# Last block of a graph network: softmax denominators inverted with nodes on partitions, self products moved into the edge loop's drain, batch statistics by rounds

## The reference, cut to what matters

```python
h = jnp.maximum(_layernorm(x, axis=-1), 0.0)
...
ex = jnp.exp(attn - amax[edge_src])
denom = jax.ops.segment_sum(ex, edge_src, num_segments=n)
alpha = ex / (denom[edge_src] + 1e-16)
upd = jax.ops.segment_sum(v * alpha[..., None], edge_src, num_segments=n)
upd = upd.reshape(n, OV) @ W_out
out = tfn_features @ W_self + upd
mu = out.mean(axis=0)
var = out.var(axis=0)
return (out - mu) * jax.lax.rsqrt(var + EPS_BN) * gamma + beta
```

## Time and profile before

| what | us |
|---|---|
| median of 3 timed runs (lowest, highest) | 3129.48 (3127.07, 3130.35) |
| span of the profiled execution, first to last instruction | 3126.1 |
| time of the profiled execution outside the span | not listed |
| busy: PE, DVE, POOL, ACT | 2476.7, 2209.2, 2032.3, 864.2 |
| from the last accumulation into acc to the end of the span | 64.3 |

### The profile page before, as it was taken

How to read it: one execution, slowest core, us unless ns; L and a number is a source line. 1 busy time by engine, 2 the same in 40 slices (tenths; PEclk the granted TensorE clock), 3 DMA queues, 4 the chain that set the end, 5 groups by cost and what they waited for, 6 DMA issues and landing times. The chain is left out here.

```text
span 3126.1 us, 51454 instructions
## 1 busy us (share of the span) xinstructions
PE 2476.7 (79%) x14006; PEld 2130.6 (68%) x14006; DVE 2209.2 (71%) x5060; ACT 864.2 (28%) x2414; POOL 2032.3 (65%) x2119
## 2 busy tenths in 40 slices
PE   5778787525667667477777767999999999999986
PEld 4777787424666666355555556888888888888862
DVE  4555555526888887555555563888888888888875
ACT  1111111136666663111111110222232222323231
POOL 4777777457777771277777736777776677677710
PEclk9776667657888888599999978999999999999985
DMA  3443333133333330155555557889888898888820
GB/s 84 94 89 86 86 87 86 30 68 64 61 60 60 60 52 4 46 155 160 152 160 152 160 147 179 214 206 214 212 206 205 203 216 206 207 204 205 213 68 11
DMA packets 333760, 404.38 MB, mean 129 GB/s; under 512 B 171136, under 2 KB 203006, under 8 KB 333570
## 3 DMA queue, kind: packets, MB, share of 16 engines
q1 hardware_dynamic: 252034, 251.20, 34.4%
q0 software_dynamic: 66560, 96.41, 14.5%
q10 hardware_dynamic: 14976, 54.53, 5.1%
HBM read 339.81 MB, written 62.07 MB: 129 GB/s over the span
## 5 line engine op out<-in xcount | busy, mean ns | idle before, releaser
L1934 PE MATMUL psum<-ckv,z 128*128 128x256 f32 x4160 | 967.8, 383 | 0.0
L1934 PEld LDWEIGHTS psum<-ckv,z 128*128 128x128 f32 x4160 | 766.7, 191 | 97.9
L1768 POOL DMA_INDIRECT acc<-QW,dst_i x416 | 399.5, 960 | 184.6 <-issue 111.2
L234 POOL DMA_INDIRECT ga<-TA,src_i x416 | 412.4, 991 | 161.6 <-issue 126.5
L1789 POOL DMA_INDIRECT ga<-XX,src_i x416 | 399.5, 960 | 162.8 <-issue 122.5
L1027 POOL DMA_INDIRECT ga<-T,src_i x416 | 401.9, 966 | 151.5 <-issue 125.9
L234 POOL DMA_INDIRECT ga<-T,src_i x416 | 396.6, 953 | 149.3 <-issue 124.7
L2048 DVE TENSOR_TENSOR z<-psum,shb 128x2560 f32<-128x2560 f32 x104 | 293.2, 2820 | 66.7 <-PE psum L1925 66.5
L1121 PE MATMUL psum<-HT,wy 128*128 128x128 f32 x1664 | 264.7, 324 | 70.0 <-DVE wy L1394 69.2
L445 PE MATMUL psum<-wre,re 128*128 128x68 f32 x832 | 215.2, 351 | 119.4 <-DVE oneT L290 67.7
L1121 PEld LDWEIGHTS psum<-HT,wy 128*128 128x128 f32 x1664 | 242.8, 232 | 87.8 <-DVE wy L1394 81.5
(11 more groups left out here) (362 smaller groups left out, 4142.9 us busy)
## 6 DMA issues: line engine op xcount, KB each, us to landing
shb<-in_ea SPq DMA_DIRECT2D x104, 640.0 KB, 6.2
WKV<-wkvo ACTq DMA_DIRECT2D x104, 512.0 KB
shb<-in_ea SPq DMA_DIRECT2D x104, 512.0 KB, 8.5
wkv<-WKV SPq DMA_DIRECT2D x104, 512.0 KB
dl<-DL SPq DMA_DIRECT2D x208, 128.0 KB
win<-TB SPq DMA_DIRECT2D x416, 32.0 KB
ga<-T,src_i POOLq DMA_INDIRECT x832
ef<-in_ea SPq DMA_DIRECT2D x104, 128.0 KB
```

The lines of the kernel that those rows point to most:

```text
L234: pool.indirect_dma_start(o, None, table, bass.IndirectOffsetOnAxis(ap=src_i[:, g * GT + t:g * GT + t + 1], axis=0)).then_inc(s_g[k], 16)
L1768: pool.indirect_dma_start(qg[:, (g % QR) * GT + t, :], None, QW, bass.IndirectOffsetOnAxis(ap=dst_i[:, g * GT + t:g * GT + t + 1], axis=0) ...
L1934: last = pe.matmul(kv_of(k)[:, t, :], z[:, k % 2, j, t * 128:(t + 1) * 128], ckv[:, j, :], start=(j == 0), stop=(j == NZ - 1))
```

## The change: what it does

The end of the fourth block is rewritten, and two things move into the edge loop's drain.

- The denominators are transposed: PE turns each of the 25 blocks of 24x125 into 125x24, with nodes on partitions (banks 1 and 7). DVE adds the three parts with one reduction per bank, adds 1e-16 and takes the reciprocal of 125x200 elements in two pieces (8 and 17 blocks). ACT writes each value 16 times in a row, round by round (`widened`), and PE transposes these blocks of 125x128 back into PSUM (banks 6 and 7), where DVE multiplies acc by them (`scaled`). sel_b, its building on POOL and its copies are gone.
- The w_self products get a bank each and are issued ahead (`own_product`): numbers 0 to 4 in the drain, at the end of PE's steps k = 1 to 5, number 5 after the reductions, number 6 in the last round. They leave the accumulation open for w_out.
- In the drain, steps without softmax work do `values` between the two halves of `add_sums`.
- DVE takes batch statistics of each round as its OT copy is done (`bn_stats`) and combines them (`bn_aggr`). A shift is worked out too, so that ACT scales and shifts OT by rounds into Y, from which PE transposes, into seven banks, without waiting for DVE's additions to X.
- ACT takes a square and a square root at the start of the end.

```diff
@@ edge loop, PE: body, and own_product ahead of it
+                def own_product(n):
+                    a, w = CH[n]
+                    if n < 2:
+                        pe.wait_ge(e3_ev, (NT // GT - 1) * 2)
+                    elif n < 4:
+                        pe.wait_ge(e3_ev, NT // GT * 2)
+                    else:
+                        pe.wait_ge(e3_z, NT // GT)
+                    pe.matmul(out_bank(n)[0:D, 0:w * PN], w_self[:], HT[:, a * PN:(a + w) * PN], start=True, stop=False)
...
+                    if i == NI and 1 <= k <= EARLY:
+                        own_product(k - 1)
@@ edge loop, DVE: body
+                    early = i == NI and val and not (p1 or p2)
+                    if early:
+                        values(*val)
                     if old:
                         add_sums(*old, 1, starts)
                     if p2:
                         split_steps(dve, S3, q, s, lambda c: fill(c, s))
-                    if val:
+                    if val and not early:
                         values(*val)
@@ the end, DVE
+                dve.tensor_reduce(rden[:, 0:DJ, :], parts(bank[1], DJ), AX.X, ALU.add).then_inc(m3_r, 1)
+                dve.wait_ge(m3_d, 2)
+                dve.tensor_reduce(rden[:, DJ:NJ, :], parts(bank[7], NJ - DJ), AX.X, ALU.add).then_inc(m3_r, 1)
...
+                c.link(dve.tensor_scalar(rden[:], rden[:], 1e-16, None, ALU.add))
+                for J in HEADS:
+                    dve.reciprocal(rden[:, J, :], rden[:, J, :]).then_inc(m3_h, 1)
...
+                def scaled(n):
+                    a, w = CH[n]
                     dve.wait_ge(m3_b, n + 1)
...
+                    dve.tensor_tensor(v, v, rbank(n)[:, 0:w * PN].rearrange("c (j p) -> c j p", j=w), ALU.mult).then_inc(m3_u, 1)
+                def statistics(n):
+                    a, w = CH[n]
+                    dve.wait_ge(m3_c, n + 1)
+                    dve.bn_stats(stats[:, n, :], OT[:, a * PN:(a + w) * PN]).then_inc(m3_dve, 1)
+                for n in range(len(CH)):
+                    scaled(n)
+                    if n > 1:
+                        statistics(n - 2)
...
+                c.link(dve.bn_aggr(bn[:, 0:2], stats[:].rearrange("f n s -> f (n s)")))
+                c.link(dve.tensor_scalar(bn[:, 3:4], bn[:, 1:2], EPS, None, ALU.add))
+                dve.wait_ge(m3_sd, 2)
                 c.link(dve.reciprocal(bn[:, 5:6], bn[:, 4:5]))
                 c.link(dve.tensor_tensor(bn[:, 6:7], bn[:, 5:6], gcol[:], ALU.mult))
-                c.link(dve.tensor_scalar(OT[:], OC[:], bn[:, 6:7], bcol[:, 0:1], ALU.mult, ALU.add))
+                c.link(dve.scalar_tensor_tensor(bn[:, 2:3], bn[:, 0:1], -1.0, bn[:, 6:7], ALU.mult, ALU.mult))
+                c.link(dve.tensor_tensor(bn[:, 7:8], bn[:, 2:3], bcol[:], ALU.add))
@@ the end, PE
+                for j in range(NJ):
+                    b, at = den_bank(j)
+                    last = pe.transpose(b[0:PN, at * 24:(at + 1) * 24], node_cols(acc[0:24, 1])[:, j, :], ident[0:24, 0:24])
...
+                def reciprocals(n):
+                    a, w = CH[n]
+                    pe.wait_ge(m3_e, n + 1)
                     if n >= 2:
                         pe.wait_ge(m3_u, n - 1)
+                    for j in range(w):
+                        last = pe.transpose(rbank(n)[:, j * PN:(j + 1) * PN], rwide[:, a + j, :], ident[0:PN, 0:PN])
+                    last.then_inc(m3_b, 1)
+                pe.wait_ge(m3_r, 2)
+                own_product(5)
+                reciprocals(0)
                 for n, (a, w) in enumerate(CH):
                     if n + 1 < len(CH):
+                        reciprocals(n + 1)
+                    if n == 6:
+                        pe.wait_ge(m3_c, 1)
+                        own_product(6)
                     pe.wait_ge(m3_u, n + 1)
+                    pe.matmul(out_bank(n)[0:D, 0:w * PN], w_out[:], node_cols(acc[:, 0])[:, a:a + w, :],
+                              start=False, stop=True).then_inc(m3_m, 1)
@@ the end, ACT
+                act.activation(bn[:, 4:5], gcol[:], ACT.Square).then_inc(m3_sd, 1)
+                act.activation(Y[:, 0:1], bn[:, 4:5], ACT.Sqrt).then_inc(m3_y, 1)
...
+                    act.activation(rwide[:, a:a + w, :].rearrange("p j (h c) -> p (j h) c", h=8),
+                                   rden[:, a:a + w, :].rearrange("p j h -> p (j h)").unsqueeze(2).to_broadcast([PN, w * 8, 16]),
+                                   ACT.Copy).then_inc(m3_e, 1)
...
+                for a, w in CH:
+                    act.activation(Y[:, a * PN:(a + w) * PN], OT[:, a * PN:(a + w) * PN], ACT.Identity,
+                                   bias=bn[:, 7:8], scale=bn[:, 6:7]).then_inc(m3_y, 1)
```

More of the change, by code:

```diff
@@ L1693, in build @@
         bcol = sb("bcol", [D, 1])
-        sel_b = sb("sel_b", [24, 128])
         XX = dram("XX", [N, 2 * D])
@@ L1743, in build @@
         sums_of = lambda half: bank[1] if half else bank[6]
+        CH = rounds(NJ, 4)
+        EARLY = 5
+        out_bank = lambda n: bank[(2, 3, 4, 5, 0, 1, 2)[n]]
         def soft_1(i, k):
@@ L1769, in queries @@
                             ap=dst_i[:, g * GT + t:g * GT + t + 1], axis=0)).then_inc(e3_gq[g % UG], 16)
[L1771 to L1781, removed]
                 pool.memset(ckv[D:128, NZ - 1, :], 0.0).then_inc(n3_p, 1)
@@ L1997, in _ @@
                 pe.wait_ge(n3_qc, len(R3))
-                pe.wait_ge(n3_p, 4)
+                pe.wait_ge(n3_p, 1)
                 pe.sem_inc(e3_S, SPARE)
@@ L2142, in build @@
         layer.close()
-        m3_r, m3_b, m3_u, m3_m, m3_c, m3_dve, m3_sd, m3_t, m3_x, m3_o, m3_s = [sem("m3_" + x) for x in
-            ("r", "b", "u", "m", "c", "dve", "sd", "t", "x", "o", "s")]
+        m3_d, m3_r, m3_h, m3_e, m3_b, m3_u, m3_m, m3_c, m3_dve, m3_sd, m3_y, m3_t, m3_x, m3_o = [sem("m3_" + x) for x in
+            ("d", "r", "h", "e", "b", "u", "m", "c", "dve", "sd", "y", "t", "x", "o")]
         OT = tmp("OT", [D, N])
[L2148 to L2151, removed]
+        Y = tmp("Y", [D, N])
+        rden = tmp("rden", [PN, NJ, 8])
+        rwide = tmp("rwide", [PN, NJ, F])
         bn = tmp("bn", [D, 8])
-        CH = rounds(NJ, 4)
-        m3_q = sem("m3_q")
+        stats = tmp("stats", [D, len(CH), 6])
+        DJ = 20
+        den_bank = lambda j: (bank[1], j) if j < DJ else (bank[7], j - DJ)
+        rbank = lambda n: bank[6 + n % 2]
+        HEADS = [slice(0, 8), slice(8, NJ)]
         with nc.Block() as block:
@@ L2158, in _ @@
                 c = Chain(dve, m3_r)
-                for n, (a, w) in enumerate(CH):
+                dve.wait_ge(m3_d, 1)
+                parts = lambda v, n: v[0:PN, 0:n * 24].rearrange("p (j a h) -> p j h a", j=n, a=3)
+                dve.tensor_reduce(rden[:, 0:DJ, :], parts(bank[1], DJ), AX.X, ALU.add).then_inc(m3_r, 1)
+                dve.wait_ge(m3_d, 2)
+                dve.tensor_reduce(rden[:, DJ:NJ, :], parts(bank[7], NJ - DJ), AX.X, ALU.add).then_inc(m3_r, 1)
+                dve.wait_ge(m3_r, 2)
@@ L2160, in _ @@
+                c.n = 2
+                c.link(dve.tensor_scalar(rden[:], rden[:], 1e-16, None, ALU.add))
[3 more added lines that the diff above has]
+                    a, w = CH[n]
                     dve.wait_ge(m3_b, n + 1)
-                    r = rden[:, n % 2, 0:w * PN]
-                    c.link(dve.tensor_scalar(r, bank[n % 2][:, 0:w * PN], 1e-16, None, ALU.add))
-                    c.link(dve.reciprocal(r, r))
@@ new lines, in _ @@
+                for n in range(len(CH)):
+                    scaled(n)
+                    if n > 1:
+                        statistics(n - 2)
+                statistics(len(CH) - 2)
+                statistics(len(CH) - 1)
+                c = Chain(dve, m3_dve)
+                c.n = len(CH)
+                dve.wait_ge(m3_dve, c.n)
+                c.link(dve.bn_aggr(bn[:, 0:2], stats[:].rearrange("f n s -> f (n s)")))
+                c.link(dve.tensor_scalar(bn[:, 3:4], bn[:, 1:2], EPS, None, ALU.add))
@@ L2174, in _ @@
+                dve.wait_ge(m3_sd, 2)
                 c.link(dve.reciprocal(bn[:, 5:6], bn[:, 4:5]))
                 c.link(dve.tensor_tensor(bn[:, 6:7], bn[:, 5:6], gcol[:], ALU.mult))
-                c.link(dve.tensor_scalar(OT[:], OC[:], bn[:, 6:7], bcol[:, 0:1], ALU.mult, ALU.add))
-                for r, (j0, n) in enumerate(rounds(NJ, 4)):
+                c.link(dve.scalar_tensor_tensor(bn[:, 2:3], bn[:, 0:1], -1.0, bn[:, 6:7], ALU.mult, ALU.mult))
+                c.link(dve.tensor_tensor(bn[:, 7:8], bn[:, 2:3], bcol[:], ALU.add))
@@ L2178, in _ @@
+                for r, (j0, n) in enumerate(CH):
                     dve.wait_ge(m3_t, r + 1)
                     dve.tensor_tensor(X[:, j0:j0 + n, :], X[:, j0:j0 + n, :],
-                                      bank[4 + r % 2][0:PN, 0:n * D].rearrange("p (j f) -> p j f", j=n), ALU.add).then_inc(m3_x, 1)
```

(57 more changed lines are left out.)

11 lines of the change are left out of this document (removed).

## The result

The changed kernel takes 3103.75 us (median of 4 runs, 3099.38 to 3104.51) against 3129.91 (4 runs, 3127.07 to 3133.78): ratio 0.9911, 95% interval 0.9900 to 0.9923. It is 26.2 us faster; 24.6 were forecast. Its profiled execution took 3103.95 with a span of 3102.2, so 1.75 lie around the span (the prediction had taken 3.4; its sum doesn't use it).

A forecast was written before the change was run, and what follows sets the result against it. The prediction took the end as one serial path, its six rounds on TensorE alone. Savings of 2.7 + 0.3 + 16.8 + 4.8 = 24.6 us off the median 3129.48 gave 3104.9, rounded to 3105, range 3099.5 to 3112.5.

The forecast's parts named there:

- Drain: Last steps of the edge loop: M3 written between the halves of the additions saves 2.7 us, bounds 0 and 5.0.
- Start: From the last accumulation to the first w_out, about 10.0 us instead of 10.27 to the first w_self: 0.3 saved.
- Rounds: Six rounds of the end on PE: 17.4 us after against 34.1 before, 16.8 saved.
- Rival A: In the shorter end TensorE's clock rises to 2.4 GHz, rounds take 1.8 us, 6.6 less: 3098; chance 0.08.
- Rival B: In the rounds VectorE becomes the bound, with bn_stats at a reciprocal's rate: 3115; chance 0.06.
- D: Slower than before: in the rounds one bn_stats between two VectorE products takes over 6.9 us; chance 0.01.
- C: The drain gives nothing back, as own products fill the gaps the earlier M3 opens: 2.7 later, 3107.6; chance 0.06.
- E: After the accumulation the chain keeps its length, the denominators' path taking 25 us instead of 10: 3120; chance 0.03.
- Batch norm: After the last OT copy, 2.5 us instead of 7.33 to the first last transposes: 4.8 saved.

The follow-up runs named there:

- e2: The changed kernel with own products 0 to 4 taken out of the drain and issued in the rounds, each ahead of its w_out: 3113.58 us.
- e1: The changed kernel with M3 of the drain written after the second half of the additions again: 3108.03 us.
- e5: The changed kernel with VectorE writing the scaled update into a tile with consecutive columns, which w_out streams instead of acc's strided ones: 3097.03 us.
- e4: The changed kernel with the denominators of before (sel_b, 500-element reciprocals on 128 partitions): 3118.94 us.
- e7: The changed kernel with M3 late, own products 0 to 4 in the rounds and the old batch norm with its table loaded early: 3117.76 us.
- run 25: Not a follow-up run: the words are a verb and a count, kernels that run 25 transposes ahead of their rounds.

## Why the prediction was right

The mechanism was the forecast one in the main, but for one short step of the drain and for a rise of the clock that the forecast left to a rival. The sum is within 1 us of the stretches (24.6 against 25.3), and some of that is luck: the start was 0.9 dearer than forecast, and the clock gave back about 1.8. By its terms:

- **Drain**, 2.7 forecast, 3.0 measured. M3 to M3 takes 4.60 and 4.61 where 4.5 was forecast, and 3.49 (3042.31 to 3045.80) where 3.4 was. The 4.5 came as forecast, from PE, which is busy 5.00 of 5.00 us there. The 3.49 is luck: this step is k = 4's, not k = 6's, since the product of one step delays the sums of the next. It isn't VectorE's own work either, which waits 1.63 for PE in it; it is short because its M3 is the first one after the softmax's steps to move ahead of the second half. The step that was meant stands in e2. All three give 2.44 from the last softmax's copy (`prow`, L628) on. The other 0.55 come from the steps k = 0 and 1, from which I had expected nothing: the distance from the last harmonics product to that copy is 26.28 instead of 26.83, and 26.82 in e1.
- **Start**, 0.3 forecast, -0.6 measured (10.27 before to the first w_self, 10.82 to the first w_out). Mis-sized: the 25 transposes of 24x125 take 6.01, not 5.31, and four spread transposes at clock 0.50 take 1.04, not 0.85. The 5.31 was a price for other operands, taken because the stride had not shown in w_out; why a 24x125 transpose is dearer wasn't tried. Own product 5 held the first of the spread transposes back, as forecast.
- **Rounds**, 16.8 forecast, 18.3 measured (34.1 before; 15.76 after, from 3070.97 to the start of the last OT copy at 3086.73). The forecast's own terms, 34.1 less 17.4, give 16.7. The first round took 3.07, where 2.9 was forecast, and the later ones 2.5, because the clock rose. At 0.50 throughout they would have taken about 17.5, an estimate from 2.05, 1.98 and 1.02 in the chain after and 1.24 for the short round in the chain before. So 17.4 was right for that clock, and the rise gave about 1.8 (17.5 less 15.76).
- **Rival A** came half true: the sign that I had set for it, a granted clock over 0.50, did come, but the price I gave it, rounds of 1.8 and 3098, did not. I had taken w_out as bound by the clock, since it stood at 1.98 beside w_self's 1.92 at 0.50. At 1.00 its strided operand holds it at 1.94, so mainly the transposes gained, about 0.45 in each of three rounds. e5 shows the rest.
- **Rival B** and **D**: bn_stats takes 0.66, as the 0.68 taken, and is hidden. **C** falls by A of the table, and e1 shows that the earlier M3 is what gives it; the products in PE-bound steps are numbers 3 and 4, where the prediction's sentence against C says 5 and 6. **E** falls by B of the table.
- **Batch norm**, 4.8 forecast, 4.4 measured: bn_aggr 0.35, and ScalarE's first scaled round with its release 0.95 (3088.96 to 3089.91) instead of 0.60. The end has one table load, at its start (below), so Identity needed none. The Trainium skill (ScalarE: Activation LUTs, Table sets: the hidden batching unit) lists identity among the functions of every set, and the trace agrees.

```profile
3060.67 1.28 ACT L2256 ACT_TABLE_LOAD   x1
```

## What to carry to other kernels

Where the tail of a kernel is one serial chain, its parts add up as long as the engine that bounds it stays the same; e4 shows the other case, in which taking 9.3 us off the engine that bounds brings 4.1, because the next engine is only a little faster: VectorE's round of 5.0 to 5.6 beside PE's 5.9. So look at that engine's round first, and shorten its work (here one reciprocal per head, spread afterwards) along with the other's. And a matmul at half clock hides the cost of a strided operand: look for it when the clock rises.

## What the runs showed of the hardware

- **Stride.** A moving operand of 500 float32 columns costs 0.98 with consecutive columns and 1.93 to 1.95 with a stride of 25 elements at granted clock 1.00, but 1.86 to 1.93 against 1.98 to 2.05 at 0.50 (changed, e2, e5). The Trainium skill (SBUF — State Buffer, Door 1: The DMA port swizzle) says that accesses that cross to a new 16-byte line pay a penalty; the pairs at 1.00 agree, and those at 0.50 show it nearly covered. No other stride was tried, so the line's size is not shown here.
- **Clock.** Rounds of w_out and 125x128 transposes lifted the clock from 0.50 to 1.00 in the first three rounds, with w_self among them (e2, e7) or without (changed). Rounds of sel_b, w_self and w_out did not, with PE busy without a gap for 23.60 us before; nor did e4's, where PE idled between (busy 7.68 of 10.00 us from 3080 to 3090). By the Trainium skill's rule (TensorE: Matmul & The Clock Gate, Part 1) a busy engine gets the full clock: the changed kernel agrees, the one before doesn't. The kernels whose clock rose also run 25 transposes ahead of their rounds, which before and e4 lack. Which of these makes the difference wasn't tried. The stretch of before:

```profile
3072.20:3095.80 23.60, 23.60 (x25) 4.18 (x25) 20.08 (x12) 2.69 (x8) 0.00 (x0) 0.50 0.00 0
```

- **Arrival.** The last harmonics product starts between 2996.42 and 3004.03 in the ten profiles, ahead of every edited line of the end, so medians of a few runs don't resolve 2 us here, while the stretches repeat to about 0.1 (A) and 0.6 (C).
